# The opening of a recurrent kernel with routed experts: inputs, first bias, weight parts and first products in another order

## What is computed

```python
def step(h, xt):
    m = concat([xt, h]) @ weight + bias          # 512 x 512
    g = sigmoid(m[:, :256] + 1.0)
    h_new = g * h + (1 - g) * tanh(m[:, 256:])
    return h_new, h_new
x = x + scan(step, cond, x)                      # 64 steps in sequence
# experts: a gate from means over steps, modulated by silu(cond) @ time_w,
# picks 2 of 4 experts for each batch; one shared expert serves all
x = x + sum(w_be * (gelu(x @ ew1 + eb1) @ ew2 + eb2)) + shared(x)
```

## Time and profile before

| | us |
|---|---|
| median of three runs | 679.57 (678.94 to 679.91) |
| the profiled execution | 680.78 |
| its span, first to last instruction | 678.7 |
| TensorE busy | 638.3 |
| VectorE busy | 421.1 |
| ScalarE busy | 311.1 |
| GpSimd busy | 266.7 |
| first tanh of the recurrence starts | 19.89 |

### The profile page before, as it was taken

The page is one execution under the profiler, slowest core; times in us unless marked ns, Lnnn a source line. Parts: engine busy times, 40 slices in busy tenths (PEclk is TensorE's granted clock), DMA queues, the critical chain, the costliest instruction groups (busy, mean ns, idle before and its releaser), DMA issues.

```text
span 678.7 us, 16806 instructions
## 1 busy us (share of the span) xinstructions
PE 638.3 (94%) x5692; PEld 550.7 (81%) x5692; DVE 421.1 (62%) x941; ACT 311.1 (46%) x518; POOL 266.7 (39%) x516
## 2 busy tenths in 40 slices
PE   3769999999999999999999999999999999999990
PEld 3668888888888888888778888888888999999980
DVE  4688876566666666677756644554447865555453
ACT  4335433343433443344546545454556654445540
POOL 2367765554544545443345233303331243333000
PEclk9999999999999999999999999999999999999995
DMA  6521100000000000000003100000002300000014
GB/s 234 188 79 49 56 24 2 1 0 0 0 0 0 0 0 0 0 2 2 0 1 94 32 0 0 0 0 0 0 0 79 110 16 0 0 0 0 0 69 180
DMA packets 7893, 20.71 MB, mean 31 GB/s; under 512 B 944, under 2 KB 1200, under 8 KB 7344
## 3 DMA queue, kind: packets, MB, share of 16 engines
q1 hardware_dynamic: 7424, 19.59, 8.6%
q10 hardware_dynamic: 432, 0.64, 0.3%
HBM read 16.03 MB, written 4.19 MB: 30 GB/s over the span
## 4 chain that ended last, share of the span: by engine, by line
PE 87%; DVE 5%; DVEq 2%; issue 2%; ACT 1%; DMA 1%; POOL 1%; ACTq 0%
PE zy L763 53%; PE hp L763 34%; DMA acc<-in_w 1%; DVE acc L706 1%; DVEq L674 1%; DVEq L694 1%; DVEq L632 1%; DVE shared_buf L635 1%; DVE d_t L476 0%; ACT uc L346 0%; DVE d_t L478 0%; DVE acc L680 0%; DVE h_b L481 0%; ACT zy L341 0%; DVE y_all L613 0%
## 5 line engine op out<-in xcount | busy, mean ns | idle before, releaser
L451 DVE TENSOR_TENSOR g_lo<-g_f,g_hi 128x512 fp32r<-128x512 f32 (+2 forms) x176 | 131.7, 749 | 119.7 <-ACT g_hi L363 116.1
L763 PE MATMUL zy<-g_hi,w_buf 128*128 128x512 f32 (+2 forms) x736 | 192.1, 382 | 0.0
L363 ACT ACTIVATE g_hi<-g_f 128x512 fp32r<-128x512 f32 (+2 forms) x184 | 113.0, 614 | 156.6 <-PE zy L763 156.4
L358 ACT ACTIVATE g_f<-hp,par 128x512 f32<-128x512 f32 (+2 forms) x184 | 123.4, 671 | 124.6 <-PE hp L763 122.3
L763 PE MATMUL hp<-shared_buf,w_buf 128*128 (+1 forms) x720 | 173.6, 376 | 1.4 <-DVE shared_buf L635 1.4
L763 PEld LDWEIGHTS hp<-shared_buf,w_buf 128*128 128x128 f32 x720 | 135.0, 188 | 20.8 <-issue 2.0
L763 PEld LDWEIGHTS zy<-g_hi,w_buf 128*128 128x128 f32 x736 | 135.2, 188 | 19.8
L763 PEld LDWEIGHTS zy<-h_b,y_all 128*128 128x128 bf16 x3072 | 93.7, 98 | 24.1 <-issue 15.6
L763 PE MATMUL zy<-g_lo,w_buf 128*128 128x512 f32 (+2 forms) x368 | 110.3, 381 | 0.0
L763 PE MATMUL zy<-h_b,y_all 128*128 128x64 bf16 x3072 | 102.2, 193 | 7.1 <-DVE h_b L481 6.3
L763 PE MATMUL hp<-x_hl,w_buf 128*128 (+1 forms) x384 | 103.2, 404 | 0.3 <-POOL x_hl L252 0.3
(11 more groups left out here) (113 smaller groups left out, 411.5 us busy)
## 6 DMA issues: line engine op xcount, KB each, us to landing
stage<-in_w_exp SPq DMA_DIRECT2D x40, 256.0 KB, 2.8
out_y<-acc SPq DMA_DIRECT2D x2, 1376.0 KB, 4.9
acc<-in_x SPq DMA_DIRECT2D x1, 2048.0 KB, 9.2
acc<-in_x SPq DMA_DIRECT2D x1, 1536.0 KB, 10.2
out_y<-acc SPq DMA_DIRECT2D x1, 1344.0 KB, 5.1
acc<-in_w SPq DMA_DIRECT2D x1, 512.0 KB, 4.7
acc<-in_x SPq DMA_DIRECT2D x1, 512.0 KB, 7.5
acc<-in_w ACTq DMA_DIRECT2D x1, 512.0 KB, 6.8
```

Of the source, the lines that this page charges most:

```text
L358: act.activation(g_f[:, j % 2, 0:n], hp[j % 2][:, 0:n], ACT.Gelu_apprx_tanh, bias=par[:, S_B1 + e * NCH + j:S_B1 + e * NCH + j + 1]).then_ ...
L363: act.activation(g_hi[:, j % 2, 0:n], g_f[:, j % 2, 0:n], ACT.Copy).then_inc(ghi_done, 1)
L451: dve.tensor_tensor(g_lo[:, j % 2, 0:n], g_f[:, j % 2, 0:n], g_hi[:, j % 2, 0:n].bitcast(F32), ALU.subtract).then_inc(glo_done, 1)
L763: return pe.matmul(out_, lhsT=lhsT, rhs=rhs, start=start, stop=stop, skip_group_check=True)
```

## The change

cond becomes the last part of `small` and lies with it in one tile, `first`; one transfer brings both. con goes to SyncE's queue behind the last x. The first bias is written by VectorE. The high part of x for steps 0 to 3 is made by GpSimd in one operation, that of steps 4 to 7 by ScalarE, and its low part by GpSimd in one operation that waits for `wh_split`. ScalarE scales and casts wh in two halves, and makes the second bf16 part as well; VectorE makes the differences. TensorE has 16 more matmuls with zeros, and takes its first products in the order in which the parts become ready (`x_first`, `h_first`). In groups 0 and 1 (`early`) the x products and their waits move by one step: none behind steps 0 and 4 of a group, two blocks behind steps 3 and 7.

```diff
+        first = sb("first", [P, S_END + 2 * K * B])
+        par = first[:, 0:S_END]
+        h_f = first[:, S_END:S_END + 2 * K * B].rearrange("p (i k b) -> p i k b", i=2, k=K)
...
             sp.dma_start(raw_w0[:, 0:K], w0[:, 0:K * 2 * D].rearrange("p (k n) -> p k n", k=K)).then_inc(s_w0, 16)
             sp.dma_start(acc[:, :, 0:GT], x[:, :, 0:GT]).then_inc(s_x0, 16)
-            sp.dma_start(con[:], consts).then_inc(s_con, 16)
             sp.dma_start(acc[:, :, GT:T // 2], x[:, :, GT:T // 2]).then_inc(s_x1, 16)
...
                     sp.wait_ge(wh_split, K)
                     sp.dma_start(acc[:, :, T // 2:T], x[:, :, T // 2:T]).then_inc(s_x2, 16)
+                    sp.dma_start(con[:], consts).then_inc(s_con, 16)
...
-            for s in range(QT, GT):
-                split_x(s, s - QT + 1)
+            pool.tensor_copy(x_hl[:, 0, :, 0:QT], acc[:, :, 0:QT]).then_inc(x0_hi, 1)
+            pool.wait_ge(x4_hi, 1)
+            pool.wait_ge(wh_split, K)
+            pool.tensor_tensor(x_hl[:, 1, :, QT:GT], acc[:, :, QT:GT], x_hl[:, 0, :, QT:GT].bitcast(F32),
+                               ALU.subtract).then_inc(xs_done, QT)
...
-            act.dma_start(h_f[:, 0], cond).then_inc(s_cond, 16)
-            act.dma_start(par[:], small).then_inc(s_par, 16)
+            act.dma_start(first[:, 0:S_END + K * B], small).then_inc(s_first, 16)
             act.dma_start(raw_w0[:, K:2 * K], w0[:, K * 2 * D:2 * K * 2 * D].rearrange("p (k n) -> p k n", k=K)).then_inc(s_w0, 16)
 
             act.wait_ge(warm_ready, 1)
             act.activation(gs[:, 64:65], gs[:, 65:66], ACT.Gelu_apprx_tanh)
-            act.wait_ge(s_cond, 16)
+            act.wait_ge(s_first, 16)
             act.activation(uc[:, 0], h_f[:, 0], ACT.Tanh, scale=0.5).then_inc(silu_t, 1)
 
             act.wait_ge(s_w0, 32)
             for k in range(K):
                 act.activation(wx[:, 0, k, 0:D], raw_w0[:, k, 0:D], ACT.Copy, scale=0.5)
                 act.activation(wx[:, 0, k, D:2 * D], raw_w0[:, k, D:2 * D], ACT.Copy).then_inc(wx_hi, 1)
+            for k in range(K):
+                act.activation(raw_w0[:, K + k, 0:D], raw_w0[:, K + k, 0:D], ACT.Copy, scale=0.5).then_inc(wh_half, 1)
+                act.wait_ge(wh_half, k + 1)
+                act.activation(wh[:, 0, k], raw_w0[:, K + k], ACT.Copy).then_inc(wh_first, 1)
+            act.wait_ge(s_x0, 16)
+            act.activation(x_hl[:, 0, :, QT:GT], acc[:, :, QT:GT], ACT.Copy).then_inc(x4_hi, 1)
+            for k in range(K):
+                act.wait_ge(wh_rest, k + 1)
+                act.activation(wh[:, 1, k], raw_w0[:, K + k], ACT.Copy).then_inc(wh_mid, 1)
+            act.wait_ge(opened, 1)
             act.wait_ge(bias_ready, 1)
-            act.wait_ge(opened, 1)
-            seed(0)
-            act.wait_ge(s_x0, 16)
-            act.activation(x_hl[:, 0, :, 0:QT], acc[:, :, 0:QT], ACT.Copy).then_inc(x0_hi, 1)
-
-            act.activation(raw_w0[:, K:2 * K, 0:D], raw_w0[:, K:2 * K, 0:D], ACT.Copy, scale=0.5).then_inc(wh_half, 1)
-            act.wait_ge(wh_half, 1)
-            act.activation(wh[:, 0], raw_w0[:, K:2 * K], ACT.Copy).then_inc(wh_first, 1)
             seed(1)
 
...
+            dve.wait_ge(bias_ready, 1)
+            dve.wait_ge(opened, 1)
+            dve.tensor_copy(zy[:, 0:2].rearrange("p a (m n) -> p (a m) n", m=K),
+                            bias_z.unsqueeze(2).to_broadcast([P, 2 * K, QT * B])).then_inc(seeded_first, 1)
 
...
-            dve.wait_ge(wh_first, 1)
             for k in range(K):
                 raw = raw_w0[:, K + k]
-                link(dve.tensor_tensor(raw, raw, wh[:, 0, k], ALU.subtract))
-                link(dve.tensor_copy(wh[:, 1, k], raw))
-                dve.tensor_tensor(wh[:, 2, k], raw, wh[:, 1, k], ALU.subtract).then_inc(wh_split, 1)
+                dve.wait_ge(wh_first, k + 1)
+                dve.tensor_tensor(raw, raw, wh[:, 0, k], ALU.subtract).then_inc(wh_rest, 1)
+            for k in range(K):
+                dve.wait_ge(wh_mid, k + 1)
+                dve.tensor_tensor(wh[:, 2, k], raw_w0[:, K + k], wh[:, 1, k], ALU.subtract).then_inc(wh_split, 1)
...
+            def x_first():
+
+                pe.wait_ge(seeded_first, 1)
+                pe.wait_ge(wx_hi, K)
+                for w, part, ready, n in ((0, 0, x0_hi, 1), (1, 0, wx_split, K), (0, 1, x0_done, 1)):
+                    pe.wait_ge(ready, n)
+                    for m in range(2 * K):
+                        o = zb[:, 0, m // 2, m % 2].rearrange("p t b -> p (t b)")
+                        for k in range(K):
+                            mm(o, wx[:, w, k, m * P:(m + 1) * P], x_hl[:, part, k, 0:QT, :], False)
+
+            def h_first():
+
+                pe.wait_ge(h3_done, 1)
+                for b, ready in enumerate((wh_first, wh_mid, wh_split)):
+                    pe.wait_ge(ready, K)
+                    for a in range(3 - b):
+                        for m in range(2 * K):
+                            for k in range(K):
+                                last = mm(zb[:, 0, m // 2, m % 2, 0, :], wh[:, b, k, m * P:(m + 1) * P], h_b[:, a, k], False, b == 2)
+                last.then_inc(z_done, 1)
+
...
-            pe.wait_ge(wx_split, K)
-            pe.wait_ge(seeded, 1)
-            pe.wait_ge(x0_done, 1)
-            for m in range(2 * K):
-                x_part(0, 0, m)
+            for i in range(16):
+                mm(hp[i % 2][:], none[:, 0:P], none[:, 0:512], True, True)
+            x_first()
             pe.wait_ge(silu_done, 1)
-            pe.wait_ge(s_par, 16)
+            pe.wait_ge(s_first, 16)
             for k in range(K):
                 last = mm(hp[0][0:B, 0:2 * E], d_t[:, k], par[:, S_TW + 2 * E * k:S_TW + 2 * E * (k + 1)], k == 0, k == K - 1)
             last.then_inc(mod_mm, 1)
-            pe.wait_ge(wh_split, K)
 
             def steps(g, filler, carry, last_group=False):
 
                 for i in range(GT):
                     s = g * GT + i
-                    h_part(s, i, i // QT)
+                    early = isinstance(g, int) and g < 2
+                    if early and s == 0:
+                        h_first()
+                    else:
+                        h_part(s, i, i // QT)
 
                     f = g - 1
                     if filler and i:
                         layer1(f, i, w_of(0), group_src(f), 512, not carry and i < 2)
                     if not (last_group and i >= QT):
-                        if i % QT == 0:
-                            pe.wait_ge(seeded, 2 * g + 2 + i // QT)
-                            pe.wait_ge(xs_done, s + QT)
-                        x_part(s - i % QT + QT, (i // QT + 1) % 2, i % QT)
+                        if i % QT == (1 if early else 0):
+                            pe.wait_ge(seeded, 2 * g + 1 + i // QT)
+                            pe.wait_ge(xs_done, s - i % QT + QT)
+                        for m in ([], [0], [1], [2, 3])[i % QT] if early else [i % QT]:
+                            x_part(s - i % QT + QT, (i // QT + 1) % 2, m)
```

More of the change, by code:

```diff
@@ L60, with cond_resid_kernel @@
 S_END = 106
-def cond_resid_kernel(nc, x, cond, w0, w_exp, small, consts, out):
+def cond_resid_kernel(nc, x, w0, w_exp, small, consts, out):
     ctx = ExitStack()
@@ L102, in cond_resid_kernel @@
         d_t = sb("d_t", [P, K, B])
-        h_f = sb("h_f", [P, 2, K, B])
+        first = sb("first", [P, S_END + 2 * K * B])
+        par = first[:, 0:S_END]
+        h_f = first[:, S_END:S_END + 2 * K * B].rearrange("p (i k b) -> p i k b", i=2, k=K)
         h_r = sb("h_r", [P, K, B])
@@ L106, in cond_resid_kernel @@
         seg = sb("seg", [P, 3, K, B])
-        par = sb("par", [P, S_END])
         con = sb("con", [P, C_END])
@@ L145, in cond_resid_kernel @@
         cmp_w = slot_w[0:B, :]
-        s_cond, s_w0, s_par, s_con, s_x0, s_x1, s_x2, s_out = (
-            sem(n) for n in ("s_cond", "s_w0", "s_par", "s_con", "s_x0", "s_x1", "s_x2", "s_out"))
+        s_first, s_w0, s_con, s_x0, s_x1, s_x2, s_out = (
+            sem(n) for n in ("s_first", "s_w0", "s_con", "s_x0", "s_x1", "s_x2", "s_out"))
         piece_in = [sem(f"piece_in{i}") for i in range(RING)]
-        wx_hi, wx_split, wh_split, bias_ready, warm_ready = (
-            sem(n) for n in ("wx_hi", "wx_split", "wh_split", "bias_ready", "warm_ready"))
-        opened, seeded = sem("opened"), sem("seeded")
-        wh_half, wh_first = sem("wh_half"), sem("wh_first")
+        wx_hi, wx_split, bias_ready, warm_ready = (
+            sem(n) for n in ("wx_hi", "wx_split", "bias_ready", "warm_ready"))
+        opened, seeded_first, seeded = sem("opened"), sem("seeded_first"), sem("seeded")
+        wh_half, wh_first, wh_rest, wh_mid, wh_split = (
+            sem(n) for n in ("wh_half", "wh_first", "wh_rest", "wh_mid", "wh_split"))
+        x4_hi = sem("x4_hi")
         piece_hi, piece_done = sem("piece_hi"), sem("piece_done")
@@ L290, in _ @@
             for i in range(GT):
-                split_x(2 * GT + i, QT + i + 1)
```

(10 more changed lines are left out.)

## The result

The changed kernel takes **675.12 us** (median of four runs, 675.06 to 675.25), beside 679.26 (678.37 to 679.91) for the one before on the same chip: a ratio of 0.9934 [0.9919, 0.9949]. The forecast was 673.1 with a range of 671.8 to 676.4: the sign was right and the time lies in the range, but 2.0 us above the forecast. Its profiled execution took 675.07, span 673.2, so 5.5 us less span than before (678.7).

A forecast was written before the change was run, and what follows sets the result against it. The prediction took the single-file opening before a never-waiting TensorE as the bound; 5.2 - 0.2 + 0.5 + 1.3 - 0.3 = 6.5 us off the profiled 680.78 gave 674.3, less 1.21 to the median 673.1, range 671.8 to 676.4.

The forecast's parts named there:

- the opening: Before step 0's cell: first tanh at 14.7 instead of 19.89 us, a gain of 5.2 us.
- GpSimd's cast: Opening: x0's high part as one 128x512 cast on GpSimd, taken as 1.2 us, from 8.5 to 9.7.
- the sum (6.5): Whole kernel: 5.2 - 0.2 + 0.5 + 1.3 - 0.3 = 6.5 us gained, from opening, GpSimd's operation and moved x products.
- w0's half: Opening transfers: w0's second half lands at 7.8 us instead of 8.50, between bounds of about 7.0 and 8.50.
- The bias on VectorE: Opening: VectorE's write of the first bias takes 1.2 us at no cost, taking 0.91 us off ScalarE's chain.
- The rival of the port: Opening: GpSimd's large cast holds up VectorE's first operation, its chain ends 1.2 us later, 674.3 us; chance 0.18.
- Piece 2: Before tanh(3): piece 2 lands late, its cast delays that tanh by some 1.6 us, 674.7 us; chance 0.07.
- GpSimd's operation off cell(0): Low parts of x4 to x7 wait for wh_split and run beside cell(0) on VectorE: a loss of 0.2 us.
- x products one step later: Groups 0 and 1: moved x products and waits gain 0.5 in step 4, 1.3 in step 8, lose 0.3 in 12.
- "+0.5" for step 4: Step 4: the wait before the x products now stands behind h_part(5), gaining 0.5 us.
- "+1.3" for step 8: Step 8: h_part(9) no longer stands behind x products waiting for GpSimd's x_low(15), gaining 1.3 us.
- The slower rival: Thin steps 0 to 7: idleness drops TensorE's rate, +1.2 us per step, 682.5 us with eight; chance 0.04.

The follow-up runs named there:

- a_olddma: Changed kernel with cond and small in two transfers again and con back ahead of x1; 676.84 us, ratio 0.9958 to the kernel before.
- a_middve: Changed kernel with the middle bf16 parts of wh given back to VectorE; 676.78 us, ratio 0.9947 to the kernel before.
- a_oldsteps: Changed kernel with the x products of groups 0 and 1 back in their old steps; 675.64 us, ratio 0.9938 to the kernel before.
- a_slot: Changed kernel with the list of slots at the start of tile seg instead of over h_f; 673.2 us, ratio 0.9903 to the kernel before.
- a_nofill: Changed kernel without the 16 products of zeros; 677.23 us, ratio 0.996 to the kernel before.
- a_slot_pad31: Changed kernel with the list of slots at the start of tile seg, plus 31 semaphore increments on VectorE in the opening; 673.18 us, ratio 0.99 to the kernel before.
- a_order: Changed kernel with TensorE waiting for all parts before its x and h products, taken in the old order; 677.09 us, ratio 0.9968 to the kernel before.
- a_seedact: Changed kernel with the first bias back on ScalarE, behind its casts of wx; 675.45 us, ratio 0.9931 to the kernel before.
- b_fill: Kernel before with the same 16 products of zeros added and nothing else; 679.78 us, ratio 0.9999 to the kernel before.

## Why the prediction was right, and where it was wrong

**The bound.** Right: the opening wins 5.74 us (5.2 were forecast), and the gain passes through all 64 steps. The experiments put prices on its parts, by how much later the first tanh comes without each: 2.2 us for the zero products, 1.8 for the order by readiness, 0.9 for the transfers, 0.2 each for the bias and for wh's middle parts. They overlap and needn't add up. GpSimd's cast of x was not tried by itself.

**Balance.** That the sum (6.5) lies so near to the lead at the last tanh (6.61) is partly luck: the opening was put 0.54 too low and GpSimd's operation at -0.2 for nothing, and against that the x products 0.63 too high (1.5 forecast; the lead grows by 0.87 behind tanh 0). Two further terms, of +1.0 and -2.1, weren't in the sum at all.

**Transfers.** w0's half was put at 7.8 between ends of 7.0 and 8.50, and landed at 6.81, below the lower end. The forecast's two causes, fewer small rows ahead of it and con out of the way, were only taken back together (a_olddma), so which of them it was isn't shown. x0 landed at 8.05 (8.5 was forecast).

**GpSimd's cast.** Scaled from four small casts it was 1.2; it took 0.61, as long as ScalarE takes for the same size (0.61 us for x4's high part, L394). A cast of a quarter of the size takes 0.29 at least, so the time doesn't grow with the size alone. The forecast multiplied it by four and had TensorE begin at 9.8; it began at 8.86. From there the forecast gave TensorE 4.8 us and it took 5.2. By the forecast's own numbers TensorE was the bound already: x products to 12.9, the gate product 0.50 and 48 h products at 1.57 make 15.0, not 14.6. The early start (0.94) less the longer row (0.4) turns 5.2 into 5.74.

**The bias on VectorE.** 1.22 us, forecast 1.2. It costs nothing next to TensorE's wait: it ends at 8.47 and x's high part at 8.71.

**The rival of the port.** Its price fell, not its mechanism. Of VectorE's four low parts the first began while GpSimd's cast ran and took 0.61 us; the others, with GpSimd idle, took 0.41. In the kernel before, with GpSimd's small operations at their side, they took 0.50 to 0.67, and x0's low part 0.83, against 0.68 alone. So the 2.0 us that the forecast took as bearing out little of the clash held some 0.6 us of it (an estimate: 2.04 less 1.62 - 0.20):

```profile
L527 DVE SCALAR_TENSOR_TENSOR shared_buf<-acc,shared_buf x4: 411/411/612, 8.4 to 9.6; 128x256 fp32r<-128x256 f32 x4
L516 DVE SCALAR_TENSOR_TENSOR shared_buf<-acc,shared_buf x4: 503/550/671, 9.3 to 10.8; 128x256 fp32r<-128x256 f32 x4
```

The first line is the changed kernel, the second the one before (ns min/median/max).

**Piece 2.** Its cast waited, in the timeline of ScalarE:

```profile
22.25 0.63 ACT L375 ACTIVATE w_buf<-stage 128x512 fp32r<-128x512 f32 x1 [0.86 <-DMA stage<-in_w_exp]
```

but it was over before tanh(3), at 24.02. The rival's wait was there, and its price was nothing.

**GpSimd's operation off cell(0).** Forecast -0.2, measured 0: tanh 0 and tanh 1 are ahead by the same 5.74. The operation took 1.27 us instead of 1.9 and ran from 13.37 to 14.64, so it was all but over when the cell began at 14.56. In a_middve it wasn't, and the cell's first operation lost 0.32 us.

**x products one step later.** This is the first step of the sum that failed. "+0.5" for step 4 held (0.57 at step 5 against a_oldsteps). "+1.3" for step 8 was right where it arises: tanh 9 is 1.31 further ahead than tanh 8. But 0.37 goes back one step later, where new waits stand in TensorE's timeline:

```profile
47.88 0.87 PE L775 MATMUL zy<-h_b,y_all 128*128 128x64 bf16 x24 [0.61 <-DVE h_b L488]
49.08 1.00 PE L775 MATMUL zy<-h_b,y_all 128*128 128x64 bf16 x24 [0.32 <-DVE h_b L475]
```

and the block itself is paid behind step 11, where 12 x products now stand in a row: the lead falls from 7.34 to 6.60. Step 12, where another block is missing, brings 0.75, and the 12 products behind step 15 take it back (6.61 at step 16). In group 1 TensorE has filler work and is nearly always busy, so a block of x products that is taken out of one step is paid in a later one. I had counted such a block as free for step 3, where there is a gap, and had not asked what it costs behind step 11, where there is none. The part is worth 0.57 us by a_oldsteps instead of 1.5.

**The way to the end.** "Nothing behind changes" was the unspoken step, and it failed twice. Slots: -2.06 us in the tail by the register load (3864 - 1807 ns), undone by a_slot. And +1.0 us where the routed batches are first gathered: between tanh 63 and TensorE's last product the lead grows from 6.61 to 7.62. Together with the sum so far, 6.61 + 1.01 - 2.13 = 5.49, the measured shift.

The gain is in one wait of TensorE, that for the gathered batches, before and after:

```profile
348.86 1.62 PE L763 MATMUL hp<-shared_buf,w_buf 128*128 128x512 f32 x6 [1.35 <-DVE shared_buf L635]
341.22 1.62 PE L775 MATMUL hp<-shared_buf,w_buf 128*128 128x512 f32 x6 [0.42 <-issue]
```

The gather is eight copies by VectorE behind a register load. Before, in the changed kernel and in a_slot:

```profile
L635 DVE CAST shared_buf<-x_hl x8: 437/450/1515, 344.6 to 348.3; 128x256 fp32r x8
L647 DVE CAST shared_buf<-x_hl x8: 450/454/1106, 336.7 to 340.0; 128x256 fp32r x8
L647 DVE CAST shared_buf<-x_hl x8: 426/452/469, 338.0 to 340.7; 128x256 fp32r x8
```

The changed kernel's last copy starts 8.3 us earlier than before: 6.6 of lead, 1.24 by the register load in front (0.87 us instead of 2.11) and 0.4 by the copies. They end near 340.5, so TensorE, which starts at 341.22, no longer waits for them.

In a_slot the load takes 2.11 us again and TensorE's wait is 0.42 all the same. There it is the copies: before, one took 1.52 us, beside a GpSimd operation of 1.39 us that starts at 345.66; in a_slot no copy is held up, and instead GpSimd's operation takes 2.97 us, which TensorE's start does not wait for:

```profile
339.30 2.97 POOL L317 TENSOR_TENSOR g_lo<-g_f,g_hi 128x512 fp32r<-128x512 f32 x1 [1.73 <-ACT g_hi L369]
```

Which of the two comes first has flipped. The Trainium skill (SBUF — State Buffer, Who interferes with whom) lists copies and casts by VectorE among the operations that can take the ports it shares with GpSimd, if they run in a mode that uses both, and says that whoever issues first has them for the whole instruction while the other is blocked. The trace before agrees, by 1.52 against 0.45 us; whether these copies run in such a mode no run shows. The flip alone gives the 1.0 us, in a_slot. The changed kernel has the flip too (the same GpSimd operation takes 2.37 us) and the shorter load besides; that the load alone would do is an estimate from its rows (336.69 + 4.10 = 340.8, ahead of 341.22) and was not tried.

**From the profiled execution to the median.** The forecast took 1.21 us off, since the median before lies that far under its profiled execution. The changed kernel has no such distance (675.07 profiled, 675.12 median). So the 1.21 couldn't be carried over from the one kernel to the other. By profiled executions the gain is 5.71 (6.5 were forecast), by medians 4.14. This conversion is the larger part of the miss: 673.1 + 0.8 + 1.2 = 675.1. The kernel before spreads over 1.5 us and its profiled executions lay at the upper edge twice (680.78, 680.71); why the changed kernel spreads over only 0.2 stays open.

**The slower rival.** Its chance of 0.04 was for all thin steps at once, and that did not happen. But its mechanism is real: the rate fell in one step in three of the profiled variants (a_nofill and a_olddma in step 5, a_middve in step 1), each time behind 1.67 or 1.83 us of idleness, and 0.6 to 1.3 us were lost by it. The changed kernel has 1.67 us in front of step 5 as well and was spared:

```profile
25.67 1.88 PE L775 MATMUL zy<-h_b,y_all 128*128 128x64 bf16 x48 [0.17 <-DVE h_b L488]
29.22 1.73 PE L775 MATMUL zy<-h_b,y_all 128*128 128x64 bf16 x48 [1.67 <-DVE h_b L488]
```

So were a_slot, a_slot_pad31, a_order, a_seedact and a_middve in that same step. What decides it isn't shown.

## What to carry to other kernels

Time won in an opening arrives at the end as long as one engine without waits stands behind it; but follow also what the edit does to data that later phases lay over the same tiles, since here one line of layout took back 2 of 7.6 us. Work that is moved out of a step in which TensorE is busy throughout is only deferred: price it where it lands. And when two engines' operations start close together, a shift of everything by some microseconds can flip which comes first, and a difference of 1 us can arise far behind the edit.

## What was unexpected of the hardware

- **A register load depends on where its data lie.** Eight values from SBUF into VectorE's registers took 1.80 and 1.81 us with the list at the beginning of a tile and 3.86 us with the list 424 bytes (106 values) into one. The load in front of the first gather goes the other way: 2.11 us in the kernel before, 0.87 in the changed one, 2.11 in a_slot. So "at the beginning of a tile" isn't the rule. Which addresses are good wasn't settled; no kernel put the list at several offsets.
- **The granted clock's column is blind before the first rise.** It read 1.00 over x products at 0.228 us each in the kernel before, and 0.50 for the same rate in b_fill, where the engine had been at its upper level before. The spacing of equal matmuls shows the level in both.
- **Idleness and the rate.** The upper level survived 2.98 us of idleness behind the zero products in a_order, did not survive 4.92 us in b_fill, and was lost in three of the eight traces that have 1.67 or 1.83 us of idleness between the h products of two steps. Idle time in front of the products alone doesn't tell it.
- **What stands ahead of a transfer.** With 117 KB as one transfer of 128 rows instead of two with 256 ahead of it, and con moved away on the other queue, the 512 KB of w0 took 1.3 us less from issue to landing (6.9 to 5.6 us, a_olddma against the changed kernel). The two weren't tried apart.
